# LoRA products of a two-layer fused block: plain float32 on 32x32 and 128x32 array tiles instead of split, masked float32r products

## The chip, the cores and the metric

The kernel runs on one core of one Trainium2 chip. The metric is the device time of one execution in microseconds.

## The reference

128 batch rows of 32 tokens with 512 features, 4096 tokens in all. Each batch row has its own two adapter numbers (one of 16, one of 64), clamped to the tables. Layer 0 is a gated feed-forward of width 1376 with rank-16 LoRA on all three matrices, scaled by 0.5, followed by a product with the signs of a weight and a bias. Layer 1 is a product of rank 16 with the adapter's pair, followed by a plain matrix with a rank-128 LoRA (its eight adapters summed) and a bias. Both layers add to the residual:

```
gate = x Wg^T + 0.5 (x Ag[i]^T) Bg[i]^T          i = adapter of the batch row
up   = x Wu^T + 0.5 (x Au[i]^T) Bu[i]^T
act  = silu(gate) * up
down = act Wd^T + 0.5 (act Ad[i]^T) Bd[i]^T
x1   = x + down sign(W0)^T + b0
out  = x1 + ((x1 B1[j]^T) A1[j]^T) (W1 + 2 sum_n w_n Bn An)^T + b1
```

The result is held to float32 accuracy, so products of float32 data are made exact in more than one pass.

## The kernel before

**Prologue.** The weights that follow `down` are folded in once on the chip: `down_sb` holds Wd^T sign(W0)^T, the table `sb_table` holds Bd sign(W0)^T for every adapter, and `c_table` holds A1 times the effective second matrix. Every float32 weight is split into a high and a low part in float32r (a float32 with a short mantissa): `wg_sb`, `wu_sb` and `down_sb` have an index of size 2 for the part. ScalarE writes the high part (`copy`, line 502) and VectorE the difference (`lo`, line 736).

**Steps.** The loop runs over 32 groups of 128 tokens, that is 4 batch rows (`GB`) each. Step g does the gate and up products of group g, the down products of group g-1 (`prev`) and the last two products of group g-2 (`pp`). The width 1376 is cut into chunks of 352, 512 and 512 columns (`CHUNKS`). Steps 0, 1 and 31 are written out, the others are a hardware loop on each engine. Nothing reorders: each engine's order is that of its `step` function, and semaphores link the engines.

**TensorE in a step** (`step`, from line 1160 on): `down(prev, 0)`, `gate` and `up` of chunk 0, `t1_product(pp)`, `down(prev, 1)`, gate of chunk 1 and so on. Each dense product of a 128-row block is three matmuls, high x high, high x low and low x high (`THREE`, line 1069).

**The LoRA products** are made dense over the four batch rows. The A vectors of the four adapters are 128 more columns beside the gate weights of chunk 0 (`wg_a`), and A_down is 64 more beside `down_sb` (`down_a`), so that each token is multiplied with all four adapters. A mask (`own_tok`) then clears what belongs to another batch row (`own_t`, `own_td`, line 795 and 816), VectorE turns the result in 32x32 pieces (lines 806 and 826), it is split again into high and low, and one matmul with 128 rows (4 batch rows x 16 ranks x high and low of B) adds the LoRA to the bank in which gate or up has accumulated (`lora`). B is fetched by GpSimd with indirect gathers (`gather_b`, line 402) into `b_raw` and split by ScalarE and VectorE into `b_sb`. Layer 1 does the same with `t1_product` (on the transposed x1, `x1T_sb`, with a sum of four quarters and a mask in `own_t1`) and `out_product`. Down has 512 + 64 = 576 columns, which don't fit in a bank of 512, so it runs in two halves of 288 in `y_ps[0]` and `y_ps[1]`.

**Transposing act.** VectorE multiplies silu(gate) by up, turns 32x32 pieces (`turn_act`), SP sends four slices from `act_sb` to `landed` (`send`), and ScalarE and VectorE split what has landed into `actT_sb`, the stationary side of down. x1 goes the same way.

**The end** (`finish`) has no further group to work under, so it transposes on TensorE and fills gaps with dummy products (`keep_busy`).

## Time and profile before

| | us |
|---|---|
| median of 3 runs | 979.64 (977.9 to 981.08) |
| profiled execution | 977.1 |
| its span, first to last instruction | 975.3 |

| engine | busy | share |
|---|---|---|
| TensorE matmul | 964.1 | 99% |
| TensorE weight load | 857.8 | 88% |
| VectorE | 736.1 | 75% |
| ScalarE | 389.1 | 40% |
| GpSimd | 371.5 | 38% |

Busy time of matmuls is a record with a modelled end, and the records of matmuls that follow each other overlap: what one costs is the distance between two starts. Weight loads run beside matmuls. HBM moves 100 GB/s over the span, of which most lies in the prologue's loads (350 GB/s in the first slices, some 120 in the loop).

### The profile page before, as it was taken

Reading aid. Unit: us, or ns where it says so; the run is one execution under the profiler, and the core shown is the slowest. Engines: PE = TensorE matmul, PEld = TensorE weight load, DVE = VectorE, ACT = ScalarE, POOL = GpSimd, SP = SyncE. Lnnn points to the kernel's source line nnn. Section 1 sums busy time; section 2 is a strip of 40 time slices with the busy share of each in tenths; the row PEclk is TensorE's granted clock in tenths of the full one; section 3 lists DMA queues with packets and bytes.
Section 4 is the critical chain, followed back from the end, with each engine's and each line's share of the span. In section 5 each row is a group of like instructions: output and inputs, shape, how many; then the busy total and the mean of one; then the engine's idle time right before and its main releaser. Section 6 shows DMA issues by size and latency. Waiting matters only on the chain.

```text
span 975.3 us, 19300 instructions
## 1 busy us (share of the span) xinstructions
PE 964.1 (99%) x5371; PEld 857.8 (88%) x5371; DVE 736.1 (75%) x1594; ACT 389.1 (40%) x669; POOL 371.5 (38%) x528
## 2 busy tenths in 40 slices
PE   9999999999999999999999999999999999999997
PEld 6788888889989988988988989899888998998996
DVE  6785787877778777777777877777787777777875
ACT  5763344343333434334343333334434333333431
POOL 1323433434444443344434333444443444444322
PEclk9999999999999999999999999999999999999999
DMA  9934444445444444544444454444445544444431
GB/s 348 378 92 118 117 129 108 126 133 135 115 117 131 115 118 130 143 109 123 126 118 114 129 140 119 124 119 130 108 126 133 137 113 119 128 119 113 130 104 44
DMA packets 155982, 128.64 MB, mean 132 GB/s; under 512 B 51648, under 2 KB 132800, under 8 KB 155840
## 3 DMA queue, kind: packets, MB, share of 16 engines
q1 hardware_dynamic: 145296, 94.37, 34.6%
q0 software_dynamic: 10672, 34.09, 12.6%
q8 instruction: 7, 0.11, 0.1%
q14 instruction: 7, 0.06, 0.0%
HBM read 86.45 MB, written 11.01 MB: 100 GB/s over the span
## 4 chain that ended last, share of the span: by engine, by line
PE 86%; DMA 4%; DVE 3%; SPq 3%; issue 2%; ACT 1%; POOL 0%; DVEq 0%; ACTq 0%; POOLq 0%
PE gu_ps L1065 54%; PE y_ps L1129 27%; DMA c_table<-rows_out 2%; PE out_ps L1065 2%; SPq L347 2%; PE t_ps L1065 1%; PE y_ps L1142 1%; DMA a_raw<-in_a 1%; PE y_ps L1065 1%; DMA landed<-act_sb 1%; DMA x_sb<-in_x 0%; SPq L317 0%; SPq L325 0%; DVE b_sb L736 0%; SPq L314 0%
## 5 line engine op out<-in xcount | busy, mean ns | idle before, releaser
L1129 PE MATMUL y_ps<-down_sb,actT_sb 128*128 128x288 f32 x2112 | 296.6, 295 | 2.6 <-DVE x_sb L838 1.3
L1129 PEld LDWEIGHTS y_ps<-down_sb,actT_sb 128*128 128x128 f32 x2112 | 288.5, 189 | 9.7 <-issue 2.9
L1065 PE MATMUL gu_ps<-wg_sb,xT_sb 128*128 128x512 f32 (+1 forms) x1152 | 274.3, 387 | 0.0
L1065 PE MATMUL gu_ps<-wu_sb,xT_sb 128*128 128x512 f32 (+1 forms) x1152 | 257.8, 368 | 0.0
L1065 PEld LDWEIGHTS gu_ps<-wg_sb,xT_sb 128*128 128x128 f32 x1152 | 211.4, 188 | 35.9
L1065 PEld LDWEIGHTS gu_ps<-wu_sb,xT_sb 128*128 128x128 f32 x1152 | 205.1, 188 | 31.3
L736 DVE TENSOR_TENSOR b_sb<-b_raw,b_sb 64x1024 fp32r<-64x1024 f32 (+2 forms) x128 | 128.4, 1003 | 72.5 <-ACT b_sb L502 59.3
L502 ACT CAST b_sb<-b_raw 64x1024 fp32r<-64x1024 f32 (+2 forms) x128 | 104.7, 818 | 103.1 <-DMA b_raw<-in_b1tab 99.6
L416 POOL TENSOR_TENSOR now<-now 128x1 int32<-128x1 int32 x160 | 46.2, 289 | 234.5 <-DVE b_sb L736 162.2
L402 POOL DMA_INDIRECT b_raw<-in_btab,now x96 | 98.3, 1024 | 79.3 <-POOL now L416 75.4
L1065 PE MATMUL gu_ps<-b_sb,tT_sb 128*128 128x512 f32 (+1 forms) x384 | 104.8, 369 | 0.0
L437 POOL TENSOR_TENSOR x_sb<-x_sb,bias_sb 128x512 f32<-128x512 f32 x31 | 46.5, 1500 | 117.9 <-DMA x_sb<-in_x 117.9
L502 ACT CAST actT_sb<-landed 128x512 fp32r<-128x512 f32 (+1 forms) x95 | 55.4, 583 | 86.7 <-DMA landed<-act_sb 86.7
L736 DVE TENSOR_TENSOR actT_sb<-landed,actT_sb 128x512 fp32r<-128x512 f32 (+1 forms) x95 | 79.5, 837 | 5.3 <-ACT actT_sb L502 4.3
L1065 PEld LDWEIGHTS gu_ps<-b_sb,tT_sb 128*128 128x128 f32 x384 | 70.0, 188 | 12.9 <-issue 0.3
L736 DVE TENSOR_TENSOR x1T_sb<-landed,x1T_sb 128x512 fp32r<-128x512 f32 x31 | 21.7, 700 | 59.4 <-ACT x1T_sb L502 57.9
L502 ACT CAST x1T_sb<-landed 128x512 fp32r<-128x512 f32 x31 | 19.2, 621 | 115.7 <-DMA landed<-act_sb 115.7
L783 DVE STREAM_TRANSPOSE act_sb<-act_sb 128x512 f32<-128x512 f32 (+1 forms) x95 | 63.1, 664 | 2.2
L445 POOL TENSOR_TENSOR xT_sb<-xT_raw,xT_sb 128x512 fp32r<-128x512 f32 x32 | 42.4, 1325 | 56.1 <-ACT xT_sb L502 56.1
L441 POOL TENSOR_TENSOR x_sb<-x_sb,bias_sb 128x512 f32<-128x512 f32 x31 | 59.1, 1906 | 12.1 <-POOL now L410 7.1
L806 DVE STREAM_TRANSPOSE tT_raw<-t_own 32x64 f32<-32x64 f32 x256 | 60.5, 236 | 4.2
L779 DVE TENSOR_TENSOR act_sb<-act_sb,gu_ps 128x512 f32<-128x512 f32 (+1 forms) x95 | 58.5, 615 | 2.7 <-PE gu_ps L1065 1.7
(171 smaller groups left out, 921.9 us busy)
## 6 DMA issues: line engine op xcount, KB each, us to landing
landed<-act_sb SPq DMA_DIRECT2D x376, 64.0 KB, 2.1
ad_raw<-in_adtab SPq DMA_DIRECT2D x128, 88.0 KB
xT_raw<-in_xT SPq DMA_DIRECT2D x32, 256.0 KB
a_raw<-in_atab SPq DMA_DIRECT2D x128, 64.0 KB
x_sb<-in_x SPq DMA_DIRECT2D x31, 256.0 KB, 3.5
out_x<-x_sb SPq DMA_DIRECT2D x31, 256.0 KB
landed<-act_sb SPq DMA_DIRECT2D x128, 48.0 KB
b_raw<-in_b1tab SPq DMA_DIRECT2D x124, 32.0 KB
```

The costliest lines, as they stand in the source:

```text
L402: nc.gpsimd.indirect_dma_start(out=dst, out_offset=None, in_=table, in_offset=bass.IndirectOffsetOnAxis(ap=index, axis=0)).then_inc(signal ...
L416: nc.gpsimd.tensor_tensor(to, row, zero, ALU.add).then_inc(L["idx"], 1)
L437: nc.gpsimd.tensor_tensor(x_sb[:], x_sb[:], bias_sb[:, 0, :], ALU.add).then_inc(L["x_biased"], 1)
L441: nc.gpsimd.tensor_tensor(x_sb[:], x_sb[:], bias_sb[:, 1, :], ALU.add).then_inc(L["x1_biased"], 1)
L445: nc.gpsimd.tensor_tensor(xT_sb[:, :, 1, :], xT_raw[:], hi(xT_sb[:, :, 0, :]), ALU.subtract).then_inc(L["xT_lo"], 1)
L502: return nc.scalar.copy(o, i)
L736: return nc.vector.tensor_tensor(o, whole, hi(high), ALU.subtract)
L779: nc.vector.tensor_tensor(a, a, gu_ps[GU_BANK[c][1]][:, 0:w], ALU.mult).then_inc(L["act_done"], 1)
L783: nc.vector.transpose(act_sb[c][:], act_sb[c][:]).then_inc(L["act_turned"], 1)
L806: turned = nc.vector.transpose(tT_raw[rows, :, tokens], t_own[tokens, :, q // 2 * QUAD:(q // 2 + 1) * QUAD])
L1065: last = nc.tensor.matmul(o, w, m, start=start and n == 0, stop=stop and n == len(terms) - 1, skip_group_check=not check)
L1129: last = nc.tensor.matmul(y_ps[half][:, 0:MH], actT_sb[:, ACTT_SLOT[c] + n, a, :], down_sb[:, blk, b, half * MH:(half + 1) * MH], start=c ...
```

## The change

All LoRA products are taken out of the dense ones and done in plain float32, in which both sides go to TensorE unsplit. Each of the four batch rows of a group has its own product that writes only its own 32 tokens, which are 32 output partitions and so one column group of the array. Hence there are no masks, and no splits of A, B, A_down, B1, c or sbd. Products with 16 ranks on the inner side have 32 rows (every second one zero, as the turned pieces are 32 wide), one row group of the array.

They come in three sessions of a step:

- `small`: t (16 products of 32 columns), td of the group before (44 of 16 columns) and t1 (16 of 16 columns), each with 128 rows and 32 output partitions, all into `small_ps`, the bank of `out_ps`.
- `first_rows`: per batch row out (512 columns), down's LoRA (512), gate and up of chunk 0 (352 each), on four row groups.
- `second_rows`: per batch row gate and up of chunks 1 and 2 (512 columns each), on four row groups. Chunk 2 reads a copy of the turned t, `lhs2_sb`, in the other half of the partitions, which SP makes by DMA.

VectorE scales the small results and turns them into `lhs_sb` (`scale_small`, `turn_small`). Down now has 512 columns in one bank. SP fetches B (`load_b`), sbd and c by plain DMAs at computed addresses; ScalarE issues the sends of chunks 0 and 1 and of x1; GpSimd keeps only the two bias additions. x1 and the output have tiles of their own. Silu of chunk 0 waits for the first session, those of chunks 1 and 2 for the second. Waits for a session stand a few dense matmuls ahead of it.

TensorE's loop before, from its start to the end of chunk 1. `down_sb` marks down, `wg_sb` and `wu_sb` gate and up, `b_sb`, `x1T_sb` and `c_sb` LoRA:

```order
248 L1129 MATMUL y_ps<-down_sb,actT_sb 128x288 x18
251 L1065 MATMUL gu_ps<-wg_sb,xT_sb 128x480 x12
252 L1065 MATMUL gu_ps<-wu_sb,xT_sb 128x352 x12
254 L1065 MATMUL t_ps<-x1T_sb,b_sb 128x256 x4
256 L1129 MATMUL y_ps<-down_sb,actT_sb 128x288 x24
258 L1065 MATMUL gu_ps<-wg_sb,xT_sb 128x512 x12
260 L1065 MATMUL gu_ps<-b_sb_60,tT_sb 128x352 x4
261 L1065 MATMUL out_ps<-c_sb,t_sb 128x512 x2
263 L1065 MATMUL gu_ps<-b_sb_61,tT_sb 128x512 x2
264 L1065 MATMUL gu_ps<-wu_sb,xT_sb 128x512 x12
```

The same stretch of TensorE's loop now, with the small session (`a_raw`, `ad_raw`, `b_raw` against untouched `xT_raw` and `landed`) and the first of the first session's four batch rows:

```order
276 L816 MATMUL y_ps<-down_sb,actT_sb 128x512 x9
278 L772 MATMUL gu_ps<-wg_sb,xT_sb 128x352 x12
279 L772 MATMUL gu_ps<-wu_sb,xT_sb 128x352 x12
287 L826 MATMUL out_ps<-a_raw,xT_raw 32x32 x16
288 L837 MATMUL out_ps<-ad_raw,landed_68 32x16 x12
289 L837 MATMUL out_ps<-ad_raw,landed_69 32x16 x16
291 L847 MATMUL out_ps<-b_raw,x_landed 32x16 x16
293 L816 MATMUL y_ps<-down_sb,actT_sb 128x512 x12
294 L772 MATMUL gu_ps<-wu_sb,xT_sb 128x512 x12
295 L872 MATMUL out_ps<-cs_rows,lhs_sb 32x512
296 L876 MATMUL y_ps<-cs_rows,lhs_sb 32x512
297 L895 MATMUL gu_ps<-b_rows,lhs_sb 32x352 x2
```

The LoRA products have moved out of gate, down and the gaps between chunks into blocks of their own, one between down of chunk 0 and down of chunk 1, one ahead of down of chunk 2, one at the end of the step. (A third row of 16 for the last chunk of td, and the rows of gate of chunk 1, are left out here.)

VectorE before, from t to td of one trip:

```order
102 L795 TENSOR_TENSOR t_own<-gu_ps,const_sb 128x128
103 L806 STREAM_TRANSPOSE tT_raw<-t_own 32x2x32 x8
104 L736 TENSOR_TENSOR c_sb<-row_raw,c_sb 64x512
105 L860 COPY t_part<-t_ps 64x128
107 L862 TENSOR_TENSOR t_part<-t_part,t_ps 64x128
109 L864 TENSOR_TENSOR t_part<-t_part,t_ps 64x128
111 L867 TENSOR_TENSOR t_sum<-t_part,const_sb 64x128 x2
112 L736 TENSOR_TENSOR tT_sb<-tT_raw,tT_sb 128x256
113 L736 TENSOR_TENSOR t_sb<-t_sum,t_sb 128x128
127 L816 TENSOR_TENSOR td_own<-y_ps,const_sb 128x64
128 L826 STREAM_TRANSPOSE tdT_raw<-td_own 32x32 x8
```

VectorE now, around the same point of a trip (`landed` and `actT_sb` are the split of the transposed act, `act_sb` the gated product):

```order
87 L586 TENSOR_TENSOR act_sb_67<-act_sb_67,gu_ps 128x512
88 L590 STREAM_TRANSPOSE act_sb_67<-act_sb_67 128x512
89 L568 TENSOR_TENSOR actT_sb<-landed_69,actT_sb 128x4x128
91 L600 TENSOR_TENSOR t_own<-out_ps,const_sb 128x64
92 L609 STREAM_TRANSPOSE lhs_sb<-t_own 32x32 x16
93 L568 TENSOR_TENSOR actT_sb<-landed_70,actT_sb 128x4x128
```

One scaling and sixteen transposes in a row now serve t, t1 and td together, where they were three separate pieces; the first session waits for the last of these transposes.

The core of the diff (TensorE's part):

```diff
@@ def gate(g, c):
-                    w += 2 * GR
@@ def step(g, prev, pp):
                 if prev is not None:
                     down(prev, 0)
                 gate(g, 0)
                 up(g, 0)
-                if pp is not None:
-                    t1_product(pp)
+                gate(g, 1, range(0, 3))
+                small_ready(g, prev, pp)
+                gate(g, 1, range(3, 4))
+                small(prev, pp)
                 if prev is not None:
                     down(prev, 1)
-                gate(g, 1)
-                lora(g, 0, 0)
-                lora(g, 0, 1)
-                if pp is not None:
-                    out_product(pp)
-                lora(g, 1, 0)
-                up(g, 1)
-                lora(g, 1, 1)
+                up(g, 1, range(0, 3))
+                first_ready(g, prev, pp)
+                up(g, 1, range(3, 4))
+                first_rows(prev, pp)
                 if prev is not None:
                     down(prev, 2)
                 gate(g, 2)
...
+                up(g, 2, range(0, 3))
+                pe.wait_ge(L["lhs2_in"], 16 * g + 16)
+                up(g, 2, range(3, 4))
+                second_rows()
```

The new products:

```python
def t_rows():
    for k in range(KC):
        for b in range(GB):
            last = nc.tensor.matmul(small_ps[tokens(b), T_AT:T_AT + T_W], xT_raw[:, k, tokens(b)],
                                    a_raw[:, b, k * T_W:(k + 1) * T_W], start=k == 0, stop=k == KC - 1,
                                    skip_group_check=True)
    return last
...
def first_rows(prev, pp):
    w = CHUNKS[0][1]
    for b in range(GB):
        if pp is not None:
            out_rows(b)                      # row group 2, bank out_ps
        if prev is not None:
            down_rows(b)                     # row group 3, bank y_ps
        for u in range(2):                   # row groups 0 and 1
            last = nc.tensor.matmul(gu_ps[GU_BANK[0][u]][tokens(b), 0:w], lhs_sb[group(u), tokens(b)],
                                    b_rows[group(u), b, 0:w], start=False, stop=True, skip_group_check=True)
    last.then_inc(L["first_mm"], 1)

def second_rows():
    for b in range(GB):
        for r in range(4):
            c, u = 1 + r // 2, r % 2
            lhs = lhs_sb if c == 1 else lhs2_sb
            last = nc.tensor.matmul(gu_ps[GU_BANK[c][u]][tokens(b), :], lhs[group(r), tokens(b)],
                                    b_rows[group(r), b, CHUNKS[0][1]:PAIR], start=False, stop=True,
                                    skip_group_check=True)
    last.then_inc(L["second_mm"], 1)
```

`td_rows` and `t1_rows` are built like `t_rows`, over 11 blocks of `landed` and 4 of `x1_landed`. In the prologue the gathers, the row indices and the masks are gone, and GpSimd clears `b_rows` and `cs_rows` (3456 and 2048 elements a partition) before SP's loop starts.

## Rows read from the trace of the kernel before

**Rows 1.** The page's first part: busy us, share of the span, instructions.
```profile
PE 964.1 (99%) x5371; PEld 857.8 (88%) x5371; DVE 736.1 (75%) x1594; ACT 389.1 (40%) x669; POOL 371.5 (38%) x528
```

**Rows 2.** Windows of three trips: stretch, length, busy per engine (count), clock, DMA share, GB/s.
```profile
560.46:588.65 28.19, 28.19 (x163) 25.44 (x161) 21.76 (x49) 10.86 (x19) 11.58 (x17) 1.00 0.46 123
588.65:616.80 28.15, 28.15 (x162) 25.31 (x161) 21.69 (x49) 10.86 (x19) 11.04 (x16) 1.00 0.45 125
616.80:645.00 28.20, 28.20 (x162) 25.47 (x161) 20.76 (x49) 10.96 (x19) 11.51 (x16) 1.00 0.47 123
```

**Rows 3.** Waits of TensorE, longest first: us in total, times, longest us.
```profile
PE y_ps L1129 <- DVE x_sb L838: 1.3, 2, 0.8
PE t_ps L1065 <- DVE x1T_sb L736: 1.2, 1, 1.2
PE gu_ps L1245 <- DVE idle_sb L965: 1.2, 1, 1.2
```

**Rows 4.** Groups by form: shapes, count | busy us, mean ns | idle.
```profile
L1065 PE MATMUL gu_ps<-wu_sb,xT_sb 128*128 128x512 f32 x768 | 191.2, 391 | 0.0
```

**Rows 5.** Timeline of TensorE in one trip: start us, length us, instruction, count.
```profile
560.46 2.76 PE L1065 MATMUL gu_ps<-wg_sb,xT_sb 128*128 128x480 f32 x12
563.05 2.08 PE L1065 MATMUL gu_ps<-wu_sb,xT_sb 128*128 128x352 f32 x12
564.98 0.64 PE L1065 MATMUL t_ps<-x1T_sb,b_sb 128*128 128x256 f32 x4
565.45 3.37 PE L1129 MATMUL y_ps<-down_sb,actT_sb 128*128 128x288 f32 x24
568.65 2.91 PE L1065 MATMUL gu_ps<-wg_sb,xT_sb 128*128 128x512 f32 x12
571.40 0.81 PE L1065 MATMUL gu_ps<-b_sb,tT_sb 128*128 128x352 f32 x4
572.04 0.62 PE L1065 MATMUL out_ps<-c_sb,t_sb 128*128 128x512 f32 x2
572.51 0.63 PE L1065 MATMUL gu_ps<-b_sb,tT_sb 128*128 128x512 f32 x2
...
583.91 0.64 PE L1142 MATMUL y_ps<-sbd_sb,tdT_sb 128*128 128x288 f32 x4
584.39 1.55 PE L1065 MATMUL gu_ps<-wu_sb,xT_sb 128*128 128x512 f32 x6
```

**Rows 6.** Timeline of the tail, matmuls and weight loads of the four transposes.
```profile
955.02 0.60 PE L1195 MATMUL gu_ps<-const_sb,xT_raw 128*128 128x128 f32 x4
955.37 1.83 PE L1129 MATMUL y_ps<-down_sb,actT_sb 128*128 128x288 f32 x12
...
954.88 0.49 PEld L1195 LDWEIGHTS gu_ps<-const_sb,xT_raw 128*128 128x128 f32 x4
```

**Rows 7.** Timeline of VectorE in the same trip.
```profile
560.18 1.22 DVE L736 TENSOR_TENSOR b_sb<-b_raw,b_sb 64x1024 fp32r<-64x1024 f32 x1
...
564.60 1.22 DVE L736 TENSOR_TENSOR b_sb<-b_raw,b_sb 64x1024 fp32r<-64x1024 f32 x1 [0.37 <-issue]
565.85 0.29 DVE L795 TENSOR_TENSOR t_own<-gu_ps,const_sb 128x128 f32<-128x128 f32 x1
...
571.74 0.69 DVE L736 TENSOR_TENSOR actT_sb<-landed,actT_sb 128x512 fp32r<-128x512 f32 x1
...
580.47 1.72 DVE L826 STREAM_TRANSPOSE tdT_raw<-td_own 32x32 f32<-32x32 f32 x8
```

**Rows 8.** Timeline of GpSimd in the same trip.
```profile
563.50 0.92 POOL L402 DMA_INDIRECT b_raw<-in_btab,now  x1 [0.80 <-POOL now L416]
...
586.73 1.30 POOL L445 TENSOR_TENSOR xT_sb<-xT_raw,xT_sb 128x512 fp32r<-128x512 f32 x1 [1.93 <-ACT xT_sb L502]
```

**Rows 9.** DMA issues: out<-in, queue, count, KB each, median us to landing.
```profile
landed<-act_sb SPq DMA_DIRECT2D x376, 64.0 KB, 2.1
```

More of the change, by code:

```diff
@@ L1127, in down @@
                     for a, b in THREE:
-                        for half in range(2):
-                            last = nc.tensor.matmul(
-                                y_ps[half][:, 0:MH], actT_sb[:, ACTT_SLOT[c] + n, a, :],
-                                down_sb[:, blk, b, half * MH:(half + 1) * MH],
-                                start=c == 0 and n == 0 and (a, b) == (0, 0),
-                                stop=c == NC - 1 and n == count - 1 and (a, b) == (1, 0))
-                if count - 1 in blocks:
-                    last.then_inc(L["down_mm"], 1)
@@ L1154, in out_product @@
-            def out_product(g):
-                pe.wait_ge(L["t1_lo"], g + 1)
-                pe.wait_ge(L["c_lo"], g + 1)
-                after(pe, L["out_done"], g)
-                product(out_ps[:], [(t1_sb[:, a, :], c_sb[:]) for a in range(2)], L["out_mm"])
+                        last = nc.tensor.matmul(y_ps[:], actT_sb[:, ACTT_SLOT[c] + n, a, :], down_sb[:, blk, b, :],
+                                                start=c == 0 and n == 0 and (a, b) == (0, 0),
+                                                stop=c == NC - 1 and n == count - 1 and (a, b) == (1, 0),
+                                                skip_group_check=True)
@@ new lines, in td_rows @@
+            def td_rows():
+                for c in range(NC):
+                    count = len(CHUNK_BLOCKS[c])
+                    for n, blk in enumerate(CHUNK_BLOCKS[c]):
+                        for b in range(GB):
+                            at = (b * count + n) * SEQ
+                            last = nc.tensor.matmul(small_ps[tokens(b), TD_AT:TD_AT + TD_W], landed[c][:, at:at + SEQ],
+                                                    ad_raw[:, b, blk * RANK:(blk + 1) * RANK],
+                                                    start=(c, n) == (0, 0), stop=(c, n) == (NC - 1, count - 1),
+                                                    skip_group_check=True)
+                return last
@@ new lines, in t1_rows @@
+            def t1_rows(by_batch=True):
+                for k in range(KC):
+                    for b in range(GB):
+                        at = (b * KC + k) * SEQ if by_batch else k * P + b * SEQ
+                        last = nc.tensor.matmul(small_ps[tokens(b), T1_AT:T1_AT + TD_W], x1_landed[:, at:at + SEQ],
+                                                b1_raw[:, b, k * RANK:(k + 1) * RANK], start=k == 0, stop=k == KC - 1,
+                                                skip_group_check=True)
+                return last
@@ new lines, in small, with out_rows @@
+            def small(prev, pp):
+                last = t_rows()
+                if prev is not None:
+                    last = td_rows()
+                if pp is not None:
+                    last = t1_rows()
+                last.then_inc(L["small_mm"], 1)
+            def out_rows(b):
+                return nc.tensor.matmul(out_ps[tokens(b), :], lhs_sb[group(2), tokens(b)], cs_rows[group(2), b, :],
+                                        start=True, stop=True, skip_group_check=True)
@@ L1309, in _ @@
             step(1, 0, None)
-            with pe.Fori(2, G - 1) as g:
+            step(2, 1, 0)
+            with pe.Fori(3, G - 1) as g:
                 step(g, g - 1, g - 2)
```

923 lines of the change are left out of this document (326 added, 597 removed).

## The prediction

> **What bounds the kernel now.** I read the page first: TensorE's matmuls are busy for 99% of the span, VectorE for 75%, ScalarE for 40%, GpSimd for 38%, and the DMA engines about half [rows 1]. Three whole trips of the loop, taken from one first `gate` to the next, last 28.19, 28.15 and 28.20 us. In each the matmuls cover the trip without a hole, at a granted clock of 1.00 (the level of 2.4 GHz) [rows 2]. TensorE's waits on another engine are short over the whole run: the largest entry is 1.3 us in two waits, then 1.2 and 1.2 in one each [rows 3]. So a step costs what its matmuls cost when lined up, and nothing else counts unless it becomes later than TensorE. A product's price is the distance to the next start, not its record (the record of a 512-column matmul is 391 ns [rows 4], since records overlap). From the order in time of one trip [rows 5]: twelve of 480 columns in 563.05 - 560.46 = 2.59 us; twelve of 352 in 564.98 - 563.05 = 1.93 us, 0.161 each; twelve of 512 in 571.40 - 568.65 = 2.75 us, 0.229 each; twenty-four of 288 in 568.65 - 565.45 = 3.20 us, 0.133 each. Set against columns at 2.4 GHz (147, 213 and 120 ns) each costs its columns plus 13 to 16 ns. I use this excess below.
>
> **What goes.** In a trip of before: 24 matmuls of gate and up for chunk 0 (2.59 + 1.93 = 4.52), 48 of 512 columns (11.00), 66 halves of down (8.80), and the LoRA products by themselves: 8 of 512 (1.83), 4 of 352 (0.64), 4 for t1 (0.47), 2 for out (0.46), 4 for down's LoRA (0.48). Sum 28.2, which is the trip. After the change the dense part is 24 x 0.161 = 3.86 (the 128 columns of A are no longer hung on the gate weights), 48 x 0.229 = 11.00, and 33 matmuls of down at 512 columns in place of 66 of 288: 33 x 0.229 = 7.56. That is 22.4 us. So 5.8 us a trip come free, and the three sessions together must cost less than that for the kernel to gain. This is the whole question.
>
> **What comes.** The order of the changed loop shows 76 small products (16 of 32 columns, 60 of 16), then 16 with 32 rows (8 of 512, 8 of 352), then 16 of 512. In the compiled program each plain float32 product is two weight loads with two matmuls, one for the low and one for the high half of the stationary side, one behind the other on the same tile. The split products of before tell what that is worth: a float32 product there is made of halves times halves, one of 0.229 us for each pair. Bounds for one plain product of 512 columns: below 0.229 (one pass), above 4 x 0.229 = 0.92 (all four pairs). I take 0.92, since the product is to be exact in both halves, and 4 x 0.161 = 0.64 for 352.
>
> *The two wide sessions.* One after another the second would cost 16 x 0.92 = 14.7 us, and the first 8 x 0.92 + 8 x 0.64 = 12.5 us: the ends from above. From below, all sixteen tiles at once, one product's length, 0.92 us each. No row shows two products side by side. I take one length plus the excess of 15 ns for each of the 32 starts, 0.92 + 0.48 = 1.4 us for each session, and keep four at once (4 x 0.92 = 3.7 us each) as the upper end of the forecast's own range.
>
> The Trainium skill (TensorE: Matmul & The Clock Gate, "Measured speedup vs the span model") has sixteen tiles of 512 columns run 10.6 times as fast as one after another; by that the second session would cost 14.7 / 10.6 = 1.4 us, an estimate from that page. The trace of before has no tile and can't bear on it, and the page does not say that it holds for plain float32.
>
> *The small session.* 76 products are 152 loads and 152 matmuls, each with few columns: at two passes a matmul, 32 or 64 columns, 13 to 27 ns of streaming, and the excess of 15 ns. A load of 128 columns is not cheaper than about 0.1 us: the four transposes of 128 columns start within 0.35 us, and their loads go on for 0.49 us [rows 6]. A quarter of that, for 32 columns, is 27 ns. So from below 152 x 0.027 = 4.1 us if only loads count and nothing runs side by side, and 38 groups of four x 0.040 = 1.5 us if the four tiles do; from above 152 x 0.107 = 16 us if a load of 32 columns costs what one of 128 does. I take 0.027 + 0.013 = 0.040 us each, 6.1 us. This is the largest term, and the one most in doubt.
>
> The Trainium skill (TensorEngine Tiling (Array Packing), "Instruction Overhead") charges about 60 cycles for any matmul, however few its columns: 25 ns at the clock of [rows 2], 152 x 0.025 = 3.8 us, an estimate from that page. With it in place of 6.1 the sum below falls by 2.3 us a trip and stays a loss. It speaks against this change, since 76 products of 16 or 32 columns are what it warns of. No row of before has a matmul under 128 columns.
>
> *Entering and leaving a session,* six times a trip: unseen. From below nothing; from above one emptying of the array each time, the part of a record past the next start, 0.391 - 0.229 = 0.16 us [rows 4, 5]. I take that: 1.0 us.
>
> Sum: 6.1 + 1.4 + 1.4 + 1.0 = 9.9, less 5.8, so +4.1 us a trip. With 31 trips +127 us.
>
> **What lies beside it.** VectorE loses its splits of B, A, A_down, B1, c and sbd, the masks and the three-step sum of t1 (1.22 + 1.22 us for two pieces of B alone [rows 7]), and gets sixteen transposes of 32x32 in a row where there were eight and eight. GpSimd loses five indirect gathers of about 0.92 us [rows 8] and keeps two additions. Neither was on the path, so this is worth nothing. One new chain matters: the end of the small session, the scaling (0.29), sixteen transposes of 1.72 / 8 = 0.215, so 3.44 [rows 7], with hand-overs about 4.0 us; then the first session. TensorE's work over it is a part of down (2.75) and nine of twelve matmuls of up (2.06), 4.8 us, as the wait stands ahead of the last three. Cover 0.8 us, if VectorE is free. If it isn't (a split of 0.69 ahead of it is late), the wait costs up to 1 us a trip. In the sum it is nothing. The second session's copied rows have a transfer of 2.1 us (as `landed<-act_sb` [rows 9]) behind 2.75 + 5.5 us of matmuls: covered. The loads of B and the two tables move to SP's queue, where they stand behind the sends of the last chunk and are wanted some 15 us later; the DMA share of about 0.45 [rows 2] leaves room. In the first step SP now waits for two GpSimd memsets of 3456 and 2048 elements a partition, perhaps 7 us at the pace of a subtraction of 512 elements in 1.30 us [rows 8], halved for want of operands, then for B: a hole of 2 to 4 us once. The tail has the same number of hand-overs.
>
> **The total.** The profiled execution took 977.1 us, its span 975.3; the median shown is 979.6, 0.25% above. 977.1 + 127 + 2 = 1106, and with the median's offset still about 1108. I say 1105.
>
> **Rivals.**
> 1. *Starts in order hold the tiles apart.* If a matmul may not start before the one ahead of it, then the high half on a tile waits until its low half has streamed, and the next tile's low half stands behind it. Then a tile costs half a product: second session 17 x 0.46 = 7.8, first 4 x (2 x 0.46 + 2 x 0.32) + 0.46 = 6.7, small 6.1, edges 1.0. Sum 21.6, +15.8 a trip, +490: 1470; with 4.1 for the small one 1405. I give the case 1440. For it: every two starts of before are in the program's order [rows 5], and low and high stand side by side in the program. Against it: a full array never had two tiles to choose from. The Trainium skill (TensorE: Matmul & The Clock Gate, "The mechanism") says that matmuls keep the program's order in start and end; that is the rule this rival would follow, and no run here shows yet whether two tiles do.
> 2. *The tiles give what they promise, so it is faster.* The place is the small session: four tiles at once there, 1.5 us, the two wide ones at 1.0, edges 0.5: 4.0, which is 1.8 under the 5.8 set free. 31 x 1.8 = 56: 923 us. It decides from the point at which the small session costs under about 2.8 us with the others at 1.4, 1.4 and 0.2, or 5.8 in all. For it: the loads overlap matmuls wholly in before (loads busy 88% beside 99% [rows 1]). Against: each of 152 starts must then cost under 18 ns, about the excess alone.
> 3. *The sum lands on 5.8 and nothing moves:* 977 us. It takes a narrow coincidence, such as the 3.8 of a small session with 0.9 + 0.9 and light edges.
> 4. *Another engine or transfer sets the trip,* a wait for `lhs_ready` or for B. Were the sessions to cost just the 5.8 us set free, this wait of up to 1 us, or 1 to 2 with a late B, would remain: 1000 to 1030 us.
>
> **How the numbers follow.** Forecast 1105, chance 0.36; its own range is 1010 (small session 4.1, edges light) to 1250 (four tiles at once in the wide sessions: 14.5 a trip, +8.7). Rival 1: 0.26. Rival 2: 0.30. Rival 3: 0.04. Rival 4: 0.04. A difference under 0.3% can't be told from none here (the three runs of before spread by 0.3%). Faster by more: 0.30; within: 0.04; slower: 0.36 + 0.26 + 0.04 = 0.66. The range reaches from 905, which leaves out the better end of rival 2 (0.07), to 1450, which leaves out the worse half of rival 1 (0.12).
>
> **What the changed kernel's profile would show.** Right: from one `gate` to the next 32 us; down with 12 matmuls of 512 columns in 2.75 us and chunk 0 with 24 in 3.86; the small session (matmuls of 32 and 16 columns) some 6 us, the two wide ones 1.4 each. Starts in order: matmuls of the wide sessions 0.46 us apart and both sessions near 7 us. Faster: the small session under 2.5 us. A wait of TensorE for `lhs_sb` or `b_rows` in each step would point to rival 4. If the dense part isn't 22.4 us, the base of the sum is wrong; if a wide plain product costs 0.23 instead of 0.92, it is the bounds.

## The result and the profile after

The changed kernel takes 982.13 us (median of 20 runs, 979.07 to 986.06); beside it on the same chip the kernel before took 978.44 us (20 runs, 975.3 to 981.08). The ratio is 1.004, 95% interval 1.0026 to 1.0053: slower by 0.4%, where +13% was forecast. The profiled execution has a span of 981.6 us. One execution of the variant `sec2` below took 3244.76 us, where its other three took 983.24 to 984.58; it is left out of that variant's time and ratio. The page's first part, which answers to [rows 1]:

```profile
PE 927.7 (95%) x10528; PEld 711.9 (73%) x10528; DVE 430.1 (44%) x1018; ACT 167.8 (17%) x287; POOL 93.4 (10%) x81
```

VectorE lost 42% of its busy time, ScalarE 57%, GpSimd 75%, and TensorE, busy for 99% before, now stands still for 5% of the span. A window of one trip, from the start of down's nine matmuls of chunk 0 to the next (columns as in [rows 2]):

```profile
562.55:590.92 28.37, 26.86 (x333) 20.74 (x322) 12.20 (x31) 3.92 (x7) 2.57 (x2) 1.00 0.49 131
```

The two after it are 28.25 and 28.33 long. A trip takes 28.3 us where it took 28.2, but matmuls cover only 26.9 of it. TensorE's waits name the rest (compare [rows 3], where nothing was over 1.3 us):

```profile
PE gu_ps L772 <- issue: 42.8, 29, 2.7
...
PE gu_ps L772 <- DMA b_rows<-in_btab: 2.7, 1, 2.7
```

One wait, 29 times, 1.5 us each. Its releaser isn't named ("issue"), so the timeline has to tell it. TensorE in one trip, as in [rows 5]:

```profile
562.55 2.34 PE L816 MATMUL y_ps<-down_sb,actT_sb 128*128 128x512 f32 x9
564.73 2.09 PE L772 MATMUL gu_ps<-wg_sb,xT_sb 128*128 128x352 f32 x12
...
568.59 2.21 PE L772 MATMUL gu_ps<-wg_sb,xT_sb 128*128 128x512 f32 x9
572.30 0.96 PE L772 MATMUL gu_ps<-wg_sb,xT_sb 128*128 128x512 f32 x3 [1.51 <-issue]
573.19 0.46 PE L826 MATMUL out_ps<-a_raw,xT_raw 128*32 128x32 f32 x32
...
574.73 3.03 PE L816 MATMUL y_ps<-down_sb,actT_sb 128*128 128x512 f32 x12
577.60 2.88 PE L772 MATMUL gu_ps<-wu_sb,xT_sb 128*128 128x512 f32 x12
580.41 0.61 PE L872 MATMUL out_ps<-cs_rows,lhs_sb 32*32 32x512 f32 x1
...
580.86 0.59 PE L872 MATMUL out_ps<-cs_rows,lhs_sb 32*32 32x512 f32 x1
...
581.47 3.01 PE L816 MATMUL y_ps<-down_sb,actT_sb 128*128 128x512 f32 x12
584.32 2.88 PE L772 MATMUL gu_ps<-wg_sb,xT_sb 128*128 128x512 f32 x12
587.04 2.88 PE L772 MATMUL gu_ps<-wu_sb,xT_sb 128*128 128x512 f32 x12
589.85 1.14 PE L904 MATMUL gu_ps<-b_rows,lhs_sb 32*32 32x512 f32 x32
590.92 2.35 PE L816 MATMUL y_ps<-down_sb,actT_sb 128*128 128x512 f32 x9
```

From start to start (a session is a block of LoRA products; the small one holds t, td and t1): the small session 574.73 - 573.19 = 1.54 us, the first 581.47 - 580.41 = 1.06, the second 590.92 - 589.85 = 1.07. Together 3.67 us for what the forecast priced at 9.9 with the edges. Twelve dense matmuls of 512 columns cost 2.72 us in the middle of dense work (584.32 to 587.04) and 2.81 to 2.87 beside a session, the nine of down behind the second one 2.18 instead of 2.04, so the edges are about 0.6 us a trip. And gate of chunk 1 takes 573.19 - 568.59 = 4.60 us instead of 2.75: a hole ahead of its last three matmuls, 1.85 us with the slower restart. That is where the small session's waits stand. SyncE (SP in the listings) in the same trip:

```profile
563.21 3.45 SPq L323 DMA_DIRECT2D cs_rows<-c_table  x4
566.86 0.43 SPq L338 DMA_DIRECT2D x_in<-in_x  x1
567.82 2.61 SPq L242 DMA_DIRECT2D landed<-act_sb  x4
571.03 3.86 SPq L300 DMA_DIRECT2D b_rows<-in_btab  x4
...
584.21 0.36 SPq L342 DMA_DIRECT2D out_x<-out_sb  x1
585.11 0.34 SPq L314 DMA_DIRECT2D ad_raw<-in_adtab  x1
585.64 0.60 SPq L315 DMA_DIRECT2D cs_rows<-sb_table  x1
```

What lies between SyncE and TensorE: VectorE in the same trip,

```profile
565.57 0.71 DVE L590 STREAM_TRANSPOSE act_sb<-act_sb 128x512 f32<-128x512 f32 x1
574.85 0.23 DVE L600 TENSOR_TENSOR t_own<-out_ps,const_sb 128x64 f32<-128x64 f32 x1 [3.29 <-PE out_ps L847]
575.11 3.45 DVE L609 STREAM_TRANSPOSE lhs_sb<-t_own 32x32 f32<-32x32 f32 x16
583.37 0.65 DVE L634 TENSOR_TENSOR out_sb<-x_sb,out_ps 128x512 f32<-128x512 f32 x1
```

the cast on ScalarE that waits for the same landing as TensorE does (`act_in2`), and so shows when it came,

```profile
571.95 0.62 ACT L424 CAST actT_sb<-landed 128x512 fp32r<-128x512 f32 x1 [1.43 <-DMA landed<-act_sb]
```

and SyncE's repeated wait, for the output ahead of the store (us in total, times, longest):

```profile
SPq L342 <- DVE out_sb L634: 21.9, 29, 3.2
```

Chunk 2 of act is turned at 566.28, but SyncE sends it only from 567.82 on. It has landed by 571.95, and TensorE goes on at 572.30. That is before the cast ends (572.57): the small session reads `landed` itself, and its wait is for the landing and not for the cast. (What the expectations below call the split on this path is not on it.) SyncE is late as it has issued four pairs for A_down and sbd, four loads of c and the load of x since 585 of the trip before (585.11 is the point that lies at 556.76 in the trip before). It could not begin them earlier, since the store ahead of them waits for the output (583.37). VectorE computes that behind chunk 0's gated product (582.32), which waits for the first session, which comes behind the small session and 5.7 us of dense work. So there is a ring: first session, gated product of chunk 0, output, store, SyncE's issues, send, landing, TensorE's wait, small session, first session. I call this **theory S**: the order and the price of SyncE's issues (some 0.8 us each: 585.11 to 586.71 for a pair, 3.86 for four of B) set the trip. **Theory T** is on the sessions: products on different tiles run side by side, each taking its own tile for about 0.9 us at 512 columns (its two matmuls start 580.86 - 580.41 = 0.45 us apart). The rivals were that the hole is TensorE's own (a price of entering a session), and that small matmuls cost their start or their weight load whatever the tile.

### The profile page after: what moved, and what is told of

It is laid out like the page before. It is cut to its first block, busy times and chain, and to the rows that moved or that the text cites. A ratio compares the mean times of both kernels' runs of the same rounds, so it can differ in the third digit from the quotient of the medians.

```text
span 981.6 us, 28045 instructions
## 1 busy us (share of the span) xinstructions
PE 927.7 (95%) x10528; PEld 711.9 (73%) x10528; DVE 430.1 (44%) x1018; ACT 167.8 (17%) x287; POOL 93.4 (10%) x81
## 4 chain that ended last, share of the span: by engine, by line
PE 93%; issue 5%; DMA 1%; POOL 0%; SPq 0%; DVE 0%; ACT 0%
PE gu_ps L772 51%; PE y_ps L816 27%; PE gu_ps L904 4%; PE out_ps L837 3%; PE out_ps L872 2%; PE y_ps L772 1%; PE out_ps L826 1%; PE gu_ps L895 1%; PE out_ps L772 1%; PE out_ps L847 1%; DMA b_rows<-in_btab 0%; DMA lb_raw<-in_lbw 0%; POOL b_rows L408 0%; PE gu_ps L934 0%; PE gu_ps L1005 0%
## 5 line engine op out<-in xcount | busy, mean ns | idle before, releaser
L816 PE MATMUL y_ps<-down_sb,actT_sb 128*128 128x512 f32 x1056 | 269.8, 403 | 0.0
L816 PEld LDWEIGHTS y_ps<-down_sb,actT_sb 128*128 128x128 f32 x1056 | 191.7, 189 | 91.1 <-issue 51.6
L609 DVE STREAM_TRANSPOSE lhs_sb<-t_own 32x32 f32<-32x32 f32 x512 | 103.9, 203 | 7.7
L435 ACT ACTIVATE act_sb<-gu_ps 128x512 f32<-128x512 f32 (+1 forms) x96 | 49.7, 552 | 324.2 <-PE gu_ps L895 302.7
L394 POOL TENSOR_TENSOR x_sb<-x_sb,bias_sb 128x512 f32<-128x512 f32 x31 | 39.8, 1284 | 475.0 <-DVE x_turn L622 475.0
L390 POOL TENSOR_TENSOR x_in<-x_in,bias_sb 128x512 f32<-128x512 f32 x32 | 41.2, 1289 | 350.7 <-DMA x_in<-in_x 350.7
L904 PE MATMUL gu_ps<-b_rows,lhs_sb 32*32 32x512 f32 x1024 | 36.6, 601 | 0.0
L876 PE MATMUL y_ps<-cs_rows,lhs_sb 32*32 32x512 f32 x256 | 35.8, 600 | 0.0
L872 PE MATMUL out_ps<-cs_rows,lhs_sb 32*32 32x512 f32 x256 | 35.8, 600 | 0.0
L837 PE MATMUL out_ps<-ad_raw,landed 128*32 128x16 f32 x2816 | 34.5, 186 | 0.0
```

The costliest lines, as they stand in the source:

```text
L390: nc.gpsimd.tensor_tensor(x_in[:], x_in[:], bias_sb[:, 0, :], ALU.add).then_inc(L["x_biased"], 1)
L435: nc.scalar.activation(act_sb[c][:, 0:w], gu_ps[GU_BANK[c][0]][:, 0:w], ACT.Silu).then_inc(L["silu_done"], 1)
L609: turned = nc.vector.transpose(lhs_sb[r * QUAD:(r + 1) * QUAD, tokens(b)], wide[tokens(b), :])
L816: last = nc.tensor.matmul(y_ps[:], actT_sb[:, ACTT_SLOT[c] + n, a, :], down_sb[:, blk, b, :], start=c == 0 and n == 0 and (a, b) == (0, 0) ...
L837: last = nc.tensor.matmul(small_ps[tokens(b), TD_AT:TD_AT + TD_W], landed[c][:, at:at + SEQ], ad_raw[:, b, blk * RANK:(blk + 1) * RANK], s ...
L872: return nc.tensor.matmul(out_ps[tokens(b), :], lhs_sb[group(2), tokens(b)], cs_rows[group(2), b, :], start=True, stop=True, skip_group_ch ...
```

## The experiments

Comparisons with before, and intervals, are of runs on the same chip. Differences between variants that ran on different chips carry what the chips differ by; the kernel before took 977.8 to 979.1 us on them.

**One issue more** (`extra`: a load of 4 KB into an unused tile at the end of SyncE's step).

```diff
+            def extra(g):
+                after(sp, L["extra"], 16 * g)
+                sp.dma_start(spare[:], consts[:, 0:8]).then_inc(L["extra"], 16)
...
                 load_x(g)
+                extra(g)
```

> The changed kernel with one more small DMA (4 KB into an unused tile) issued by SP in each step, behind the load of x. Theory S: SP's issues are in the ring, each costs 0.9 us with its gap, so the trip grows by 0.6 to 1.0 us and the kernel by 19 to 31 us, to 1001 to 1013. Rival R1: SP has nothing to do with the hole, 982 us.

Measured 1019.84 us, ratio to before 1.0423 (1.0402 to 1.0444). 38 us over the changed kernel for 32 small loads, 1.2 us each, more than the 0.6 to 1.0 expected. TensorE in one trip:

```profile
591.02 1.45 PE L779 MATMUL gu_ps<-wg_sb,xT_sb 128*128 128x512 f32 x3 [1.98 <-issue]
```

and two windows behind the hole (the three matmuls, the small session; columns as in [rows 2], the clock third from the end):

```profile
591.02:592.39 1.37, 1.37 (x3) 0.62 (x3) 0.00 (x0) 0.25 (x1) 0.00 (x0) 0.59 0.73 174
592.39:594.60 2.21, 2.21 (x154) 2.17 (x153) 0.00 (x0) 0.00 (x0) 0.00 (x0) 0.50 0.64 199
```

The hole has grown from 1.5 to 1.98 us, and behind it the granted clock falls to 0.50, the level of 1.2 GHz, in some trips: three matmuls take 1.37 us from start to start instead of 0.89, the small session 594.55 - 592.39 = 2.16 instead of 1.54. These 1.1 us lie in the ring. The mean clock of the run is 0.965, where the changed kernel has 0.994. The same trace separates the two causes. From the end of one hole to the end of the next:

```profile
562.21:591.02 28.81, 26.83 (x322) 20.74 (x322) 12.23 (x30) 3.93 (x8) 2.57 (x2) 1.00 0.49 129
591.02:621.02 30.00, 28.02 (x321) 21.52 (x322) 12.23 (x30) 3.95 (x8) 2.56 (x2) 0.94 0.48 124
```

A trip at a clock of 1.00 is 0.5 us longer than the changed kernel's 28.3, one behind whose hole the clock falls is 1.7 us longer, and about one trip in three is of the first kind. So the issue itself costs some 0.5 us a trip, a little under theory S's 0.6 to 1.0, and the larger part of the 38 us is the clock's. (`e_before` below, the same load in the kernel before at a clock of 0.999, costs 0.8 us a step.)

**More of TensorE's work** (`sec2`: the second session twice, so that the LoRA of chunks 1 and 2 is added twice).

```diff
-                for b in range(GB):
+                for b in [*range(GB), *range(GB)]:
```

> The changed kernel with the sixteen products of the second session done twice (the LoRA of chunks 1 and 2 is added twice). Theory S: the second session lies outside the ring, in the stretch that waits for SP anyway. SP is free for the last send 1.0 us after that chunk is turned, so 1.0 us more on TensorE is swallowed by the hole: 982 to 990 us. Rival R2 (TensorE sets the trip and the hole is part of its price): +1.0 x 32, 1014 us.

Measured 983.49 us, 1.0053 (1.0032 to 1.0073). The work is there (TensorE's timeline),

```profile
587.29 2.35 PE L904 MATMUL gu_ps<-b_rows,lhs_sb 32*32 32x512 f32 x64
589.57 2.33 PE L816 MATMUL y_ps<-down_sb,actT_sb 128*128 128x512 f32 x9
```

and the wait shrinks by it:

```profile
PE gu_ps L772 <- issue: 9.7, 27, 0.7
```

1.2 us more of matmuls a trip cost 1.4 us in the whole kernel. TensorE doesn't bound the changed kernel, and the second session isn't in the ring.

**SyncE relieved** (`a1`: the store and the load of x are issued by GpSimd; SyncE's next loads wait for the first session's products, their real need, and `load_b1` goes ahead of that wait).

```diff
@@ SyncE's step
-                if pp is not None:
-                    store(pp)
...
-                load_x(g)
@@ GpSimd's loop
+                load_x(g + 1)
+                store(g - 1)
```

> The changed kernel with SP relieved: GpSimd issues the load of x and the store of the output, and SP's loads of A_down, sbd and c wait for the first session itself instead of standing behind the store (which waits for VectorE's addition). Theory S (the trip is set by the ring first session -> silu, gated, addition -> store -> some 16 us of SP's DMA issues -> send of the last chunk -> small session): SP is through with its loads before the last chunk is turned, the hole of 1.85 us a trip ahead of the small session goes, a trip is 26.5 us and the kernel about 982 - 29 x 1.85 = 928 us. Rival R1 (the hole is what a session costs to enter, or the act chain is that long by itself): the hole stays, 982 us.

Measured 945.5 us, 0.9649 (0.9628 to 0.967): 3.5% faster than before. What is left of the hole, as a wait and in the timeline:

```profile
PE gu_ps L777 <- issue: 6.8, 27, 1.5
```

```profile
579.60 0.96 PE L777 MATMUL gu_ps<-wg_sb,xT_sb 128*128 128x512 f32 x3 [0.27 <-issue]
```

Theory S holds in sign and place. The size falls short of the 928 us expected, as 0.27 us and the restart remain.

**Both** (`a1_sec2`: a1 with the second session twice, the same edit as sec2).

> As a1, with the second session's sixteen products done twice (the LoRA of chunks 1 and 2 is added twice). Theory S: without the hole TensorE sets the trip, so here the same doubling shows in full: 16 plain float32 products of 512 columns on sixteen tiles cost 0.9 to 1.07 us a step, +29 to +34 us over a1. If the tiles started in order (rival 1 of the prediction) it would be +7 us a step, over +200. If a1 keeps its hole, it is swallowed here too: 0 to +8 over a1.

Measured 976.8 us, 0.9982 (0.9972 to 0.9993), 31 us over a1. The same 1.2 us a trip (37 us in all) that cost 1.4 us in the changed kernel now cost 31: with SyncE relieved, the second session counts. It counts in either of two ways, as TensorE's own work or as the start of the chain called theory C below, and this run doesn't tell them apart.

**SyncE relieved further** (`b1`: a1 with the load of x transposed on GpSimd's queue too, and the copy of lhs on ScalarE's).

```diff
@@ SyncE's step
-                    load_xT(nxt)
-                copy_lhs(g)
@@ GpSimd's loop
                 add_bias0(g)
+                load_xT(g + 1)
                 add_bias1(g)
                 load_x(g + 1)
@@ ScalarE's step
+                act.wait_ge(L["lhs_ready"], g + 1)
+                act.dma_start(lhs2_sb[2 * QUAD:P, :], lhs_sb[0:2 * QUAD, :]).then_inc(L["lhs2_in"], 16)
```

> As a1, and SP relieved further: GpSimd issues the load of xT too, ScalarE the copy of the turned rows; A_down, sbd and c are guarded by their own waits. Theory S: in a1 SP is busy for 27.15 us of a trip of 27.1 and so still sets it; here it has some 25.1 us of issues, TensorE becomes the bound with 26.6 us a trip and no hole: 945.5 - 31 x 0.5 = 930 us. Rival R3 (the 0.27 to 0.5 us left in a1 is the act chain's own length, or the array's price of entering the small session): 944 to 946 us.

Measured 1104.25 us, 1.1299 (1.1276 to 1.1321): a miss, and my own doing. TensorE's longest wait and its place in one trip:

```profile
PE gu_ps L782 <- DVE xT_sb L578: 109.1, 30, 4.1
```

```profile
563.11 3.89 PE L782 MATMUL gu_ps<-wg_sb,xT_sb 128*128 128x352 f32 x12 [3.56 <-DVE xT_sb L578]
```

GpSimd in the same trip:

```profile
586.44 0.56 POOL L389 DMA_DIRECT2D x_in<-in_x  x1
...
590.33 1.29 POOL L377 TENSOR_TENSOR x_in<-x_in,bias_sb 128x512 f32<-128x512 f32 x1 [2.79 <-DMA x_in<-in_x]
591.56 0.55 POOL L385 DMA_DIRECT2D xT_raw<-in_xT  x1
```

The load of xT stands behind the addition to x_in, which waits for x, which is loaded only when the addition to x1 is done (586.44): a new ring through a queue in which each instruction is cheap. Each hole of 3.6 us costs a second time: the twelve matmuls behind it have a record of 3.89 us instead of 2.09, at a granted clock of 0.50, and that of the run is 0.933.

**Tiles, measured inside b1.** Three variants of b1. `b1_same` takes chunk 2's product on chunk 1's rows, so that its output holds chunk 1's LoRA in place of chunk 2's:

```diff
-                        lhs = lhs_sb if c == 1 else lhs2_sb
-                        last = nc.tensor.matmul(gu_ps[GU_BANK[c][u]][tokens(b), :], lhs[group(r), tokens(b)],
-                                                b_rows[group(r), b, CHUNKS[0][1]:PAIR], start=False, stop=True,
+                        last = nc.tensor.matmul(gu_ps[GU_BANK[c][u]][tokens(b), :], lhs_sb[group(u), tokens(b)],
+                                                b_rows[group(u), b, CHUNKS[0][1]:PAIR], start=False, stop=True,
```

> As b1, but in the second session chunk 2 uses the rows and the tiles of chunk 1 (it adds chunk 1's LoRA to chunk 2), so 8 tiles take two products each where 16 take one. Theory T (a product occupies its own tile for four passes, 0.86 us, and different tiles run side by side): +0.86 us a step, +27 us. Theory O (what counts is the number of starts, whatever the tile): 0. Theory Q (only row groups run side by side, not column groups): no change from the mix, since the four column groups stay as they are; two row groups in place of four would double the session, +1.1, +34 us.

`b1_batch` has the small session batch row by batch row, one column tile at a time (here t; td and t1 likewise):

```diff
-                for k in range(KC):
-                    for b in range(GB):
+                for b in range(GB):
+                    for k in range(KC):
```

> As b1, but the small session runs batch row by batch row: all products of one column group follow each other (4, 11 and 4 of them) before the next column group has its turn. Theory F (TensorE looks a few instructions ahead at most, and a full tile holds up those behind it): the overlap is lost but at the borders between batch rows, so 152 matmuls at 39 ns each come to 5 to 6 us instead of 1.54: +3.5 to +4.5 us a step, +108 to +140 us. Theory N (each tile has a queue of its own deep enough): 0 to +10 us.

`b1_td2` issues the 44 products of td twice in the small session:

```diff
                     last = td_rows()
+                    last = td_rows()
```

> As b1, with the 44 products of td done twice, which gives the same result. Theory P (the price of a small product on four tiles in turn is what the trace shows, 19.5 ns for a product and its two halves): 44 x 0.0195 = +0.86 us a step, +27 us. If part of the small session's 1.54 us is entering and leaving: less than that. The prediction's price of 0.080 a product would give +3.5 us, +109 us.

Measured 1095.61 (1.1199, 1.1151 to 1.1246), 1165.82 (1.1918, 1.1889 to 1.1946) and 1145.39 us (1.172, 1.1699 to 1.1741). Against b1 that is -9, +62 and +41 us, where +27, +108 to +140 and +27 were expected. These times say little, as the ring of b1 and its falls of the clock lie over them; b1_same is even below b1. The sessions themselves can be read, as the second one of b1_same in TensorE's timeline:

```profile
587.50 1.99 PE L913 MATMUL gu_ps<-b_rows,lhs_sb 32*32 32x512 f32 x32
589.41 0.96 PE L826 MATMUL y_ps<-down_sb,actT_sb 128*128 128x512 f32 x3
```

Two products on a tile make the second session 589.41 - 587.50 = 1.91 us instead of 1.07, +0.84, at a clock of 1.00. In b1_batch the small session goes from 1.54 to 3.81 us, 25 ns for each of 152 matmuls instead of 10. In b1_td2 it is 2.29 us, 88 more matmuls in 0.75 us, 8.5 ns each.

**The order on GpSimd mended** (`b2`: xT is loaded one round of GpSimd's loop earlier; `b2_same` and `b2_batch` are the edits above on it).

```diff
-            with pool.Fori(1, G - 1) as g:
+            with pool.Fori(1, G - 2) as g:
                 add_bias0(g)
-                load_xT(g + 1)
+                load_xT(g + 2)
                 add_bias1(g)
```

(What the first expectation calls subtractions are these two additions of the biases.)

> a1 with the load of the next step's x (transposed) also off SyncE's queue, now on GpSimd's between the subtraction of chunk 0 and that of chunk 1, so that it is issued when the small session has ended, and the copy of lhs into lhs2 on ScalarE's queue. SyncE then issues 12 DMAs a trip (eight of A and B, four of the tables) instead of 14. Theory S (SyncE's issue queue sets the trip): in a1 SyncE was busy 27.15 of 27.12 us a trip and a hole of 0.27 us was left; without two issues TensorE sets the trip: 22.4 of dense work + 1.54 + 2 x 1.07 + some 0.3 of starts = 26.4 to 26.8 us, 0.3 to 0.7 less than a1, so 924 to 936 us, no wait of TensorE over 0.1 us a trip. Rival: what is left in a1's trip is no queue of SyncE's but the chain through the activation's transposes, or GpSimd's queue closes a new ring: 943 us or more, and a wait that is named on TensorE.

> b2 with chunk 2's LoRA product taken on the row groups (and with the numbers of B and lhs) of chunk 1: it computes chunk 1's LoRA twice and chunk 2's not at all. The second session's 16 products then stand two on each of 8 tiles, instead of one on each of 16. Theory T (each product takes its tile for 0.86 us or so and tiles run side by side): the second session goes from 1.07 to 1.9 us, and with no wait on SyncE the whole kernel pays for it: +0.84 x 32 = +27 us over b2. Rival (the products queue one behind another at the array's input, whatever their tile): no change, within 3 us of b2.

> b2 with the small session's 152 matmuls ordered batch row by batch row: 38 on one column tile, then 38 on the next, instead of the four tiles in turn. Theory T: the tiles no longer run side by side, the session goes from 1.54 to 3.8 us (as it took in b1's version), and the kernel pays 2.27 x 31 = +70 us over b2. Rival (what a small matmul takes is its start at the array's input and not its tile): within 5 us of b2.

Measured: b2 948.05 us, 0.969 (0.9665 to 0.9716), as fast as a1 or a little slower, though SyncE has two issues fewer (28 a trip instead of 30; the 12 and 14 of the expectation are miscounted): the rival's case. b2_same 972.57 us, 0.9928 (0.9908 to 0.9947), +24.5 over b2 where 27 was expected; b2_batch 1015.3 us, 1.0371 (1.0347 to 1.0395), +67 where 70 was. Theory T holds in time as well as in the trace: with TensorE almost unheld, the whole kernel pays what a session costs more. b1_same's rival that only row groups run side by side is out too: b2_batch changes nothing but the order of the column tiles. In b2_batch the small session lies between these two starts of TensorE's timeline, 3.82 us apart:

```profile
558.02 0.80 PE L841 MATMUL out_ps<-a_raw,xT_raw 128*32 128x32 f32 x29
...
561.84 1.43 PE L831 MATMUL y_ps<-down_sb,actT_sb 128*128 128x512 f32 x5
```

In b2 the hole of a1 is still there (timeline of TensorE), while SyncE, which issued almost without a rest in a1, has a new long wait, for the turned act of the chunk it is to send:

```profile
578.00 0.95 PE L787 MATMUL gu_ps<-wg_sb,xT_sb 128*128 128x512 f32 x3 [0.26 <-issue]
```

```profile
SPq L242 <- DVE act_sb L605: 48.6, 30, 5.5
```

It waits some 1.5 us a trip, where the changed kernel had sent 1.5 us late. And ScalarE's cast of chunk 2, which waits for the same landing, starts 0.36 us ahead of TensorE's three matmuls in a1 (579.24) and in b2 (577.64), as in the changed kernel (0.35). So the remainder should be the chain of chunk 2 itself (second session, silu, product, turn, send, landing), **theory C**, and no queue; the next pair tests it.

**The wait moved** (`b2_late` and `c_late`: on b2 and on the changed kernel itself, the small session's waits stand behind the last three matmuls of gate instead of ahead of them).

```diff
                 gate(g, 1, range(0, 3))
-                small_ready(g, prev, pp)
                 gate(g, 1, range(3, 4))
+                small_ready(g, prev, pp)
```

> b2 with TensorE's waits for the small session (the last chunk of act landed and split, among others) moved from ahead of the last three matmuls of gate of chunk 1 to behind them, right ahead of the small session. Theory C (what is left in a1 and b2 is the chain from the second session through silu, gated product, turn, send and split of chunk 2 to these waits, late by 0.26 us a trip, whatever SyncE does): three matmuls now cover it, so the hole of 0.26 goes and with it the slow restart after it (three matmuls 0.89 us apart instead of 0.69). Trip 27.14 - 0.23 - 0.20 = 26.7 us, 933 to 938 us, 10 to 14 us below b2. Rival: something else holds TensorE once a trip (its own queue, a fixed cost of entering the session), the gap moves with the wait or stays: within 3 us of b2.

> The changed kernel with nothing but that wait moved behind the last three matmuls of gate of chunk 1. Theory S (a ring of first session, store, SyncE's 10 issues ahead of the send of the last chunk, its landing, the split, the wait, the small session and down and up of chunk 1 sets the trip): the ring gets shorter by the three matmuls, 0.69 to 0.9 us, until SyncE's own 27.6 busy us a trip hold it. Trip 28.37 - 0.75 = 27.6, so 955 to 962 us. Rival (the hole is a delay of fixed size that follows from what TensorE itself does there, or only the chain from the second session counts): the hole of 1.5 us shrinks by nothing, within 5 us of the changed kernel's 982.

Measured: b2_late 933.01 us, 0.9534 (0.9511 to 0.9556), 15 under b2; c_late 959.52 us, 0.9801 (0.9775 to 0.9828), 23 under the changed kernel. A trip of b2_late, without a hole (columns as in [rows 2]):

```profile
588.71:615.30 26.59, 26.59 (x333) 20.80 (x322) 11.86 (x31) 3.92 (x7) 4.17 (x5) 1.00 0.54 140
```

TensorE of c_late:

```profile
587.12 0.46 PE L826 MATMUL out_ps<-a_raw,xT_raw 128*32 128x32 f32 x32 [0.83 <-issue]
```

and SyncE there, one load of xT and the next, and its wait for the output:

```profile
562.46 0.37 SPq L333 DMA_DIRECT2D xT_raw<-in_xT  x1
...
589.96 0.37 SPq L333 DMA_DIRECT2D xT_raw<-in_xT  x1
```

```profile
SPq L342 <- DVE out_sb L634: 5.8, 2, 3.0
```

Both theories stand. In c_late the ring is shorter by three matmuls, and the wait for the output on SyncE falls from 21.9 to 5.8 us over the run; SyncE now issues without a rest, one trip of it being 27.5 us, the trip's own length. In b2_late TensorE doesn't wait in the loop, and the trip is what it has to do. The three matmuls that moved would cover any wait of that size, so b2_late shows that the remainder stood at these waits; that it was chunk 2's landing is read from the times above. This version beats both kernels, by 4.7% and by 5%.

**Had SyncE slack before?** (`e_before`: the kernel before with the same extra load as in `extra`.)

```diff
                 send_act(g, 1)
                 if prev is not None:
                     send_x1(prev)
+                extra(g)
```

> The kernel before with one more DMA of 4 KB a step on SyncE's queue, behind the send of x1 (the same that cost the changed kernel 38 us). If SyncE's queue was covered before and became the bound by the change: no more than 0.3% over before, 979 to 982 us, and no wait of TensorE of note. Rival: SyncE's queue was at its limit in before too, where TensorE and it tied: +0.5 to 1.2 us a trip, 995 to 1017 us.

Measured 1004.48 us, 1.0262 (1.024 to 1.0283), so the rival's case. TensorE's longest wait and one place of it:

```profile
PE y_ps L1136 <- DVE x_sb L845: 19.4, 29, 1.3
```

```profile
602.49 2.55 PE L1136 MATMUL y_ps<-down_sb,actT_sb 128*128 128x288 f32 x18 [0.55 <-DVE x_sb L845]
```

My expectation, that the change had used up a slack, is wrong. The kernel before stood at a tie: TensorE full, and a second ring through SyncE (load of x, residual sum, `y_ps` free for down) so close behind it that one issue more a step costs 26 us, 0.8 us each. That the ring runs through the load of x is read from this wait; no run moved that load.

## Why the forecast was wrong

- **The dense part, 22.4 us a trip: right.** 352 columns at 1.93 for twelve, 512 at 2.72, down in 2.85 to 2.87 with its edge. The 5.8 us are free.
- **The two wide sessions, 1.4 us each: nearly right.** Measured 1.07. The term of one product's length, 0.92 from four halves, is borne out by b1_same (0.84 for a second product on the same tile). The 15 ns a start was too much: 1.07 - 0.84 leaves 0.23 us for 32 starts. By the Trainium skill (TensorE: Matmul & The Clock Gate, "Measured speedup vs the span model") it would have been 1.4 too, an estimate; here sixteen products of 0.84 in 1.07 us are 12.6 times the pace of one tile.
- **The small session, 6.1 us: the step that failed by the most.** It measured 1.54 us. I priced each of 152 matmuls at 0.040, a load and a start in a row, and took the lower end "38 groups of four" as a bound only. Two errors lie in it. One after another on one tile they cost 25 ns (3.82 us in b2_batch), not 40. And the four column tiles do run side by side, 10 ns each. The 60 cycles of the Trainium skill (TensorEngine Tiling (Array Packing), "Instruction Overhead"), 3.8 us by my estimate, are just what one tile at a time takes, so the trace agrees with the page there; with four tiles in turn it doesn't hold per matmul.
- **Edges, 1.0 us: too high,** about 0.6 by the dense groups beside a session.
- With these three terms mended the sum is 3.7 + 0.6 = 4.3 against 5.8, rival 2's case and nearly its number: -1.5 a trip, some 932 us. b2_late, the sum with TensorE not waiting, is 933.
- **"The DMA share leaves room": the second failed step,** of the other sign. I looked at the transfers' time and not at the queue that issues them. The change takes twelve sends off SyncE and gives it twelve table loads (B, sbd, c), so that it has 32 issues a trip as it had 31, now with the chunk that the next session needs behind fourteen others, of which the first waits for the output. That is 1.85 us a trip. It is rival 4's kind (a transfer sets the trip), but in another place than the two I named, `lhs_ready` and B. These were right as costing nothing: scaling and transposes end 3.8 us after the small session (4.0 forecast), and the first session starts 1.9 us later.
- **Rival 1, starts in order: wrong.** Each product is one call in the kernel and two matmuls in the trace. The first ones of the four tiles of `out` start from 580.41, the second ones from 580.86, with matmuls of products that are called later between. The rule the rival leaned on in the Trainium skill (TensorE: Matmul & The Clock Gate, "The mechanism"), that matmuls keep the program's order in start, doesn't fit this trace if the two matmuls of a product stand side by side in the compiled program, as the prediction says; the trace doesn't show that order. The same bears on "nothing reorders" in the section on the kernel before: for starts on different tiles this trace doesn't bear it out.
- **Rival 3, nothing moves, 977 us: nearly the number, for another reason.** It took the sessions to cost the 5.8 us set free. They cost 4.3, which frees 1.5 us a trip, and one wait takes some 1.85. That the two nearly cancel is luck, and so is the sign: the forecast was slower for the sessions' price, and the kernel is slower for a wait that the sum had at nothing.
- **The first step's hole, 2 to 4 us: right,** 2.7 us for `b_rows`, once.

So 0.4% is no sign that the change does little: some 46 us gained on TensorE (b2_late against the kernel before), and as much lost again in one wait.

## What to carry to other kernels

When a change frees time on the bounding engine, ask what comes second, and count for each queue that issues DMAs its issues times their price, not only the bytes; the order on the queue is part of the dependence graph, since an issue that waits holds all behind it. Adding one tiny DMA to a kernel shows how much cover that queue has, before anything is rewritten; the clock of its trips has to be read beside the time, as it took the larger part here. A wait belongs right ahead of the work that needs it, unless it is known to be early.

## What the runs showed of the hardware

- Plain float32 products of 512 columns on sixteen 32x32 tiles: 1.07 us for all, 0.84 more for a second on each tile ([rows 5] gives 0.229 for one full-array matmul).
- Small matmuls (16 or 32 columns, 32 output partitions): 25 ns each on one column tile, 10 ns on four in turn, 8.5 ns for more of the same. Whether the load or the matmul holds the tile, no run separates.
- An issue of SyncE costs 0.76 (a_raw, four in 3.04) to 0.97 us (B, four in 3.86); a load of 4 KB cost the kernel before 0.8 us a step, and the changed kernel 0.5 us in a trip at full clock, so small ones are not free.
- Twelve matmuls behind a hole of 3.56 us ran at half pace (record 3.89 instead of 2.09 us); the clock there was 0.50. Behind a hole of 1.51 us it stayed at 1.00 (572.30 to 574.73 in the changed kernel), behind holes of about that of `extra` (1.98 us) it fell in about two trips of three.
